# Softmax attention's head: the other heads' rows are stored after the first group's loads have landed

## The chip, the cores and the metric

One core of one Trainium2 chip runs the whole program. The metric is device time in microseconds (us) of one execution, lower being better; the time of a version is the median of several executions.

## The reference

The program is a chain of two layers, each attention and then a mixture of experts, on 2048 rows of 128 numbers. Only the second layer's attention is touched by the change. Cut to what matters:

```python
x = x + _L1_attn_ref(_layernorm(x, axis=-1), L1_attn_Wq, ...)
...
scale = 1.0 / np.sqrt(HD)
scores = jnp.einsum('bhsd,bhed->bhse', q, k) * scale
attn = jax.nn.softmax(scores, axis=-1)
out = jnp.einsum('bhse,bhed->bhsd', attn, v)
out = out.transpose(0, 2, 1, 3).reshape(b, l, e)
return out @ Wo.T + bo
```

Here q, k and v are x times a weight of 128 x 128 plus a bias, cut into 16 heads of 8 numbers, q and k turned by position-dependent angles (rope); x has 2 sequences of 1024 rows.

## The kernel before

The program runs four stages one after the other, with a barrier of all engines between them: delta-rule attention, experts, softmax attention, experts. The softmax attention lies in the profile from about 424 us to 809 us. `attn1_pe`, `attn1_dve`, `attn1_act`, `attn1_pool` and `attn1_sp` each write the instructions of one engine in the order in which it runs them; nothing is rescheduled. The engines meet at semaphores.

**The units.** q and k of 2048 positions are made in 8 units (`UNITS1`) of 512 positions each; unit 0 is k of positions 0 to 511, unit 1 is k of 512 to 1023, unit 2 is q of 0 to 511, unit 3 is q of 512 to 1023, all of the first sequence. Units 4 to 7 belong to the second sequence. Each value is cut into three bf16 thirds (semaphores `a1_h0`, `a1_h1`, `a1_r2` or `a1_r2d` say that a third is there), in the buffer `a1_part`, which has four slots: unit 4 writes where unit 0 lay, so ScalarE's `leading(4)` (line 1106) first waits until unit 0's stores have landed (line 1102).

**Through memory and back.** A unit has 16 heads by 8 numbers on the partitions; the score products want the 7 pair rows of a head on the partitions instead. SyncE (SP) therefore stores each third to a scratch tensor in main memory (`store`, line 1276) and loads it back in the other order (`load`, line 1283). The first group is heads 0 to 3: 32 partitions of each unit. The other heads are 96 partitions. The first FIRST = 3 units are stored in these two pieces, with semaphores `a1_sf0` to `a1_sf2` for the first group and `a1_st0` to `a1_st2` for the others; unit 3 goes as one piece. What a DMA queue holds is worked on in the background, but SP itself stands still at each `wait_ge`, and everything behind that wait in its program stands still too.

**SP's order before.** The nine stores of the first group, with two stores of the others' unit 0 among them; the three loads of the first group for maxima (224 KB each, semaphore `a1_first`); the remaining seven stores of the others' units 0 to 2; three stores of unit 3; then a wait for unit 3's stores, its load (`a1_second`), a wait for `a1_st0` to `a1_st2`, and eight loads of 448 KB (`a1_two0`, `a1_one1`, `a1_two1`, `a1_one2`; line 1283). Then `max_rows(0)`: four small stores of row maxima to `scr_m` (line 1295), a wait until they have landed, and a load of them into row positions of q (line 1297, semaphore `a1_mrow0`). Behind that come six more group loads and the stores of units 4 to 7.

**The loops.** TensorE computes 256 tiles of scores only for their row maxima (`max_half`, line 903, two products each; the first waits for `a1_first`), VectorE reduces each (line 1019). The first 26 tiles (AHEAD) run alone. From then on TensorE interleaves two tiles of maxima with four products of scores (`scores`, line 922) and, from the third unit on, eight products with the values (`values`, line 933). ScalarE takes the exponentials (line 1158). The maxima of 16 tiles are split by GpSimd (`split_rows`, lines 1227 to 1234) and turned by VectorE (line 1026, once after tile 19 and then every 16 tiles) for `max_rows`. The first `scores` waits for `a1_two0` and `a1_mrow0`.

Of the kernel before, what the change touches and what calls it, by code (L numbers as in the profile page):

```python
# [788 lines left out]
FIRST = 3  # L789
# [467 lines left out]
def attn1_sp(c):  # L1257
    nc, sp, m, S = c.nc, c.sp, c.mem, c.sem
    q, kk, mt = m["a1_q"], m["a1_k"], m["a1_mt"]
    scr = [nc.dram_tensor(f"scr_{n}", [NH, HD, PAIRS, T], BF16, kind="Internal").ap() for n in "qk"]  # L1260
    scr_m = nc.dram_tensor("scr_m", [2, 3, HG * 4, 4, 32], BF16, kind="Internal").ap()

    def store(n, third, heads, sem):

        what, b = UNITS1[n]
        if third < 2:
            sp.wait_ge(S(("a1_h0", "a1_h1")[third]), n + 1)
        elif n in DVE_UNITS:
            sp.wait_ge(S("a1_r2d"), n)
        else:  # L1270
            sp.wait_ge(S("a1_r2"), 1 if n == 0 else n - 1)
        at = slice(heads[0] * HD, heads[1] * HD)
        to = scr[what].rearrange("h d r t -> (h d) r t")[at, :, b * BLK:(b + 1) * BLK]
        rows = to[:, 3 * third:min(3 * third + 3, PAIRS), :] if what == 0 else to[:, third:PAIRS:3, :]
        part = m["a1_part"][at, n % 4, third, :].unsqueeze(1).broadcast_to([rows.shape[0], rows.shape[1], BLK])
        sp.dma_start(rows, part).then_inc(S(f"{sem}{n}"), 16)

    def store_all(n):
        for third in range(3):
            store(n, third, (0, NH), "a1_st")  # L1280

    def load(what, base, k, at, to, sem):
        sp.dma_start((q, kk)[what][base:base + KR, k, :, to],
                     scr[what][k * HG:(k + 1) * HG, :, :, at].rearrange("h d r t -> (d r) h t")).then_inc(S(sem), 16)

    def group(base, g, name):
        k, b = g % NG, g // NG
        for what in (1, 0):
            load(what, base, k, slice(b * L, (b + 1) * L), slice(0, L), name)

    def max_rows(e):
        g, qh = e // 2, e % 2
        sp.wait_ge(S("a1_mc"), e + 1)
        for r in range(4):
            sp.dma_start(scr_m[qh, :, :, r, :].rearrange("a i j -> i a j"), mt[32 * r:32 * r + 16]).then_inc(S("a1_ms"), 16)
        sp.wait_ge(S("a1_ms"), 64 * (e + 1))
        sp.dma_start(q[KR:KA, g % NG, :, qh * BLK:(qh + 1) * BLK],
                     scr_m[qh].rearrange("a (h t) r j -> a h (t r j)", h=HG)).then_inc(S(f"a1_mrow{qh}"), 16)

    block = [slice(b * BLK, (b + 1) * BLK) for b in range(QH)]  # L1300
    first, others = (0, HG), (HG, NH)
    for n in range(FIRST):
        for third in range(3):
            store(n, third, first, "a1_sf")
            if n == 0 and third < 2:
                store(n, third, others, "a1_st")
    for n in range(FIRST):
        sp.wait_ge(S(f"a1_sf{n}"), 48)
        what, b = UNITS1[n]
        load(what, S1B, 0, block[b], block[b], "a1_first")  # L1310
    store(0, 2, others, "a1_st")
    for n in range(1, FIRST):
        for third in range(3):
            store(n, third, others, "a1_st")
    store_all(3)
    sp.wait_ge(S("a1_st3"), 48)
    load(0, S1B, 0, block[1], block[1], "a1_second")
    for n in range(FIRST):
        sp.wait_ge(S(f"a1_st{n}"), 48)
    for g in range(NG):  # L1320
        group(0, g, f"a1_two{g}")
        if g + 1 < NG:
            group(S1B, g + 1, f"a1_one{g + 1}")
        if g == 1:
            max_rows(0)
    for n in range(4, 7):
        store_all(n)
    max_rows(1)
    store_all(7)
    max_rows(2)  # L1330
    for e in range(3, 2 * G):
        max_rows(e)
        if e == 3:
            for n in range(4, 8):
                sp.wait_ge(S(f"a1_st{n}"), 48)
        if e % 2 == 1 and e // 2 + 3 < G:
            g = e // 2 + 3
            sp.wait_ge(S("a1_s1"), 32 * (g - NG + 1))
            group(S1B, g, f"a1_one{g}")
            sp.wait_ge(S("a1_pv"), U * (g - NG + 1))  # L1340
            group(0, g, f"a1_two{g}")
    for qh in range(2):
        sp.wait_ge(S(f"a1_mrow{qh}"), 16 * G)


def attn1(c, w, x):
    attn1_sp(c)
    attn1_pe(c)
    attn1_act(c, x)
    attn1_dve(c, x)  # L1350
    attn1_pool(c, x)
    tables_sp(c, w, "f1", 1)
# [1232 lines left out]
```

## Time and profile before

| | us |
|---|---|
| three runs, median | 916.6 |
| three runs, lowest and highest | 915.05 and 917.56 |
| the profiled execution, its own time | 918.17 |
| the profiled execution, span from first to last instruction | 916.8 |
| VectorE busy | 689.2 (75% of the span) |
| TensorE busy | 747.2 (82%) |
| ScalarE busy | 499.5 (54%) |
| mean granted clock of TensorE | 0.887 of full speed |

The profiled execution took 918.17 us, of which 916.8 us are its span; that is 1.57 us above the median of the runs. The shares are averages over four stages with different limits, so what follows reads the stage of the change by itself. Positions such as "475.84" are microseconds from the start of the span.

### The profile page before, as it was taken

The numbers are of one execution on the slowest core, as the hardware profiler recorded it, in microseconds if no ns is written. First come the engines' busy times: TensorE is split into PE (matmuls) and PEld (weight loads), VectorE is DVE, ScalarE is ACT, GpSimd is POOL, SyncE is SP. The second block draws the span as 40 slices with busy tenths as digits, with TensorE's granted clock in tenths as the row PEclk, the third lists the DMA queues.
The fourth block names the chain that finished last, engine by engine and source line by source line (L and its number), as shares of the span: only waits on it lengthen the run. The fifth ranks groups of instructions, "written<-read, shape, count | busy, mean of one in ns | idle before, by whom it ended". The sixth has DMA issues, their size and how long they took to land. (4 is left out here: it accounts for less than half of the span.)

```text
span 916.8 us, 18626 instructions
## 1 busy us (share of the span) xinstructions
PE 747.2 (82%) x7061; PEld 364.4 (40%) x7062; DVE 689.2 (75%) x1378; ACT 499.5 (54%) x989; POOL 245.0 (27%) x297
## 2 busy tenths in 40 slices
PE   6999978988418999945887999999999999936880
PEld 3343256643317999943211222222222222225770
DVE  7868964457784555538796999999999998865765
ACT  4744412655403343434435888888888889821223
POOL 0130010323035666661552200000000100005773
PEclk9999979976658999977857999999999999956995
DMA  3530010000461111231878030303120000041113
GB/s 95 118 68 3 1 25 5 4 1 0 172 219 38 45 45 45 44 107 36 222 156 231 2 73 12 82 3 83 33 51 3 2 2 4 9 159 32 50 47 98
DMA packets 40624, 55.60 MB, mean 61 GB/s; under 512 B 12552, under 2 KB 28048, under 8 KB 39896
## 3 DMA queue, kind: packets, MB, share of 16 engines
q1 hardware_dynamic: 36568, 46.28, 18.8%
q0 software_dynamic: 3968, 8.13, 3.1%
q8 instruction: 57, 0.93, 0.4%
q14 instruction: 31, 0.25, 0.1%
HBM read 35.45 MB, written 14.75 MB: 55 GB/s over the span
## 5 line engine op out<-in xcount | busy, mean ns | idle before, releaser
L1019 DVE TENSOR_REDUCE arena<-psum 128x1 f32<-128x1024 f32 x256 | 300.7, 1216 | 24.0 <-PE psum L903 21.2
L1158 ACT ACTIVATE arena<-psum 128x512 f32<-128x512 f32 x512 | 265.9, 605 | 53.8 <-PE psum L922 53.7
L903 PE MATMUL psum<-arena 56*128 56x512 bf16 x512 | 179.2, 409 | 11.8 <-DVE arena L1019 10.2
L922 PE MATMUL psum<-arena 59*128 59x512 bf16 x512 | 155.8, 388 | 5.9 <-ACT arena L1158 3.7
L933 PE MATMUL psum<-arena 128*32 128x512 f32 x1024 | 138.1, 611 | 8.7 <-issue 8.7
L370 PE MATMUL psum<-arena 128*128 128x128 f32 x808 | 110.9, 290 | 7.9 <-DVE arena L424 7.2
L370 PEld LDWEIGHTS psum<-arena 128*128 128x128 f32 x808 | 99.0, 198 | 19.4 <-DVE arena L424 19.4
L922 PEld LDWEIGHTS psum<-arena 59*128 59x128 bf16 x512 | 38.3, 94 | 166.4 <-ACT arena L1158 141.3
L475 POOL DMA_INDIRECT rows_y<-arena x62 | 62.1, 1001 | 47.7 <-DVE arena L429 43.1
L1227 POOL TENSOR_SCALAR arena<-arena 128x16 f32<-128x16 f32 x16 | 4.1, 254 | 249.2 <-DVE arena L1019 249.0
L470 POOL DMA_INDIRECT arena<-rows_x,arena x62 | 60.9, 982 | 31.6 <-issue 16.8
L391 PE MATMUL psum<-arena 128*128 (+1 forms) x496 | 66.5, 278 | 0.9 <-ACT arena L454 0.8
L903 PEld LDWEIGHTS psum<-arena 56*128 56x128 bf16 x512 | 37.5, 95 | 71.3 <-DVE arena L1019 69.1
L391 PEld LDWEIGHTS psum<-arena 128*128 128x128 f32 x496 | 61.1, 194 | 1.2 <-DVE arena L429 0.9
L451 ACT ACTIVATE arena<-psum 128x512 f32<-128x512 f32 x39 | 23.3, 597 | 59.6 <-PE psum L370 59.6
L416 DVE TENSOR_TENSOR arena<-arena,psum 128x512 f32<-128x512 f32 x39 | 26.8, 686 | 33.4 <-PE psum L370 33.4
L412 DVE COPY arena<-arena 128x512 f32 x62 | 27.3, 440 | 26.6 <-issue 26.1
L448 ACT COPY arena<-arena 128x512 f32 x39 | 24.1, 619 | 34.8 <-DVE arena L303 19.5
L2242 PE MATMUL psum<-arena 128*32 128x512 f32 x352 | 40.8, 593 | 0.2 <-DMA arena<-arena 0.2
L933 PEld LDWEIGHTS psum<-arena 128*32 128x32 f32 x1024 | 20.6, 108 | 42.0 <-issue 38.5
L454 ACT ACTIVATE arena<-arena 128x512 f32<-128x512 f32 x23 | 14.5, 630 | 40.2 <-DVE arena L420 40.2
L1982 ACT ACTIVATE arena<-psum 128x64 f32<-128x64 f32 x32 | 7.2, 224 | 41.8 <-PE psum L2264 41.7
(316 smaller groups left out, 1068.0 us busy)
## 6 DMA issues: line engine op xcount, KB each, us to landing
arena<-scr_k SPq DMA_DIRECT2D x15, 448.0 KB
arena<-scr_q SPq DMA_DIRECT2D x15, 448.0 KB
arena<-in_f_up SPq DMA_DIRECT2D x1, 4096.0 KB, 13.8
arena<-rows_y SPq DMA_DIRECT2D x12, 256.0 KB, 5.5
scr_q<-arena SPq DMA_DIRECT2D x6, 384.0 KB, 3.8
arena<-in_f_down SPq DMA_DIRECT2D x1, 2048.0 KB, 20.1
rows_x<-xn SPq DMA_DIRECT2D x2, 1024.0 KB, 15.4
arena<-in_f_up SPq DMA_DIRECT2D x1, 2048.0 KB, 10.2
```

Of the source, the lines that this page charges most:

```text
L370: mm = pe.matmul(ps[:, bank, f * P:(f + 1) * P], w[:, a.pair, at], xt[:, a.pair, :], start=True, stop=True)
L391: mm = pe.matmul(ps[:, 5 + 2 * d.pair, 0:P], h[:, d.pair, f * P:(f + 1) * P], merged(wdown[:, ed, f * P:(f + 1) * P]), start=f == 0, stop= ...
L412: dve.tensor_copy(m["e_w"][:, x0.pair, 0:F], merged(m["e_up"][:, bass.ds(e, 1), 0:F])).then_inc(picked, 1)
L416: dve.tensor_tensor(h[:, u.pair, :], sg[:, u.pair, :], ps[:, 2 + u.pair, :], ALU.mult).then_inc(hidden, 1)
L470: pool.indirect_dma_start(xs[:, t % SLOTS, :], None, src, index).then_inc(landed[t % SLOTS], 16)
L475: pool.indirect_dma_start(dst, index, y[:, d.slot, :], None).then_inc(stored[d.slot], 16)
L903: mm = pe.matmul(ps[:, bank + half, :], q[rows, k, h, (qh * 4 + qt) * P:(qh * 4 + qt + 1) * P], kk[rows, k, h, half * BLK:(half + 1) * BLK ...
L922: pe.matmul(ps[:, score_bank(n), :], kk[0:KA, k, h, kb * P:(kb + 1) * P], q[0:KA, k, h, qh * BLK:(qh + 1) * BLK], start=True, stop=True).t ...
L933: mm = pe.matmul(ps[32 * h:32 * h + 32, 7, :], va[:, kb, (st % NG) * HG + h, :], pt[:, (u % 3) * HG + h, :], start=kb == 0, stop=kb == NTB ...
L1019: dve.tensor_reduce(mx[:, qh, h * 4 + qt:h * 4 + qt + 1], ps[:, bank:bank + 2, :].rearrange("p a b -> p (a b)"), X, ALU.max).then_inc(S("a ...
L1158: act.activation(pt[:, (u % 3) * HG + h, :], ps[:, score_bank(n), :], ACT.Exp, scale=float(HD) ** -0.5).then_inc(S("a1_exp"), 1)
L2242: mm = pe.matmul(ps[32 * h:32 * h + 32, fir_bank(n, i), :], m["a0_wfir"][:, (g0 + g) * H0 + h, :], v4[:, h, b, PAD + t0 - 4 * g:PAD + t0 - ...
```

## The change

The two stores of the other heads' unit 0 that lay among the first group's stores are taken out and put behind the loads, and SP waits for `a1_first` to reach 48, that is for all three loads of the first group to have landed, before it issues the first of these nine stores.

```diff
     for n in range(FIRST):
         for third in range(3):
             store(n, third, first, "a1_sf")
-            if n == 0 and third < 2:
-                store(n, third, others, "a1_st")
     for n in range(FIRST):
         sp.wait_ge(S(f"a1_sf{n}"), 48)
         what, b = UNITS1[n]
         load(what, S1B, 0, block[b], block[b], "a1_first")
-    store(0, 2, others, "a1_st")
-    for n in range(1, FIRST):
+    sp.wait_ge(S("a1_first"), 3 * 16)
+    for n in range(FIRST):
         for third in range(3):
             store(n, third, others, "a1_st")
     store_all(3)
```

No instruction of TensorE, VectorE, ScalarE or GpSimd changes or moves. On SP the beginning of the stage changes like this (line, transfer, partitions x pair rows x positions, and the semaphores waited for ahead of it; 32 partitions are the first group, 96 the others):

```order
 L1276 DMA scr_k<-arena 32x3x512 [waits barrier_Pool_Activation_PE_DVE_SP_release,a1_h0]
-L1276 DMA scr_k<-arena 96x3x512 [waits a1_h0]
 L1276 DMA scr_k<-arena 32x2x512 [waits a1_h1]
-L1276 DMA scr_k<-arena 96x2x512 [waits a1_h1]
 L1276 DMA scr_k<-arena 32x2x512 [waits a1_r2]
 L1276 DMA scr_k<-arena 32x3x512 [waits a1_h0]
```

The two stores of 96 partitions leave the place between the first group's; the nine stores of 32 partitions now follow one another. Behind the three loads SP's program has this:

```order
 L1283 DMA arena<-scr_k 56x4x512 [waits a1_sf1]
 L1283 DMA arena<-scr_q 56x4x512 [waits a1_sf2]
+L1276 DMA scr_k<-arena 96x3x512 [waits a1_h0,a1_first]
+L1276 DMA scr_k<-arena 96x2x512 [waits a1_h1]
 L1276 DMA scr_k<-arena 96x2x512 [waits a1_r2]
 L1276 DMA scr_k<-arena 96x3x512 [waits a1_h0]
```

The same two stores stand there now, the first of them behind the wait for `a1_first`, and all that follows in SP's program is behind that wait as well: twelve stores (nine of 96 partitions, three of 128) where ten stood, then the loads of the groups.

## Rows read from the trace of the kernel before

**Rows 1.** The page, part 5: busy, mean ns of one, idle before it.

```profile
L1019 DVE TENSOR_REDUCE arena<-psum 128x1 f32<-128x1024 f32 x256 | 300.7, 1216 | 24.0 <-PE psum L903 21.2
```

**Rows 2.** Windows: busy of PE, PEld, DVE, ACT, POOL; PEclk; DMA share; GB/s.

```profile
560.00:600.00 40.00, 38.17 (x261) 8.75 (x257) 38.15 (x35) 34.23 (x67) 2.89 (x11) 1.00 0.23 48
```

**Rows 3.** Timeline at the first scores: start, us, engine, line; idle before, releaser.

```profile
475.84 0.58 PE L922 MATMUL psum<-arena 59*128 59x512 bf16 x1 [2.07 <-DMA arena<-scr_m]
...
476.93 1.22 DVE L1019 TENSOR_REDUCE arena<-psum 128x1 f32<-128x1024 f32 x1 [1.89 <-PE psum L903]
```

**Rows 4.** Timeline of the SP queue: start, us of issuing, line, tensors, count.

```profile
437.51 0.88 SPq L1283 DMA_DIRECT2D arena<-scr_k  x2
438.64 0.31 SPq L1283 DMA_DIRECT2D arena<-scr_q  x1
438.99 2.96 SPq L1276 DMA_DIRECT2D scr_k<-arena  x4
442.00 4.51 SPq L1276 DMA_DIRECT2D scr_q<-arena  x6
449.76 0.33 SPq L1283 DMA_DIRECT2D arena<-scr_q  x1
...
468.12 1.71 SPq L1295 DMA_DIRECT2D scr_m<-arena  x4
473.33 0.84 SPq L1297 DMA_DIRECT2D arena<-scr_m  x1
...
500.59 1.52 SPq L1276 DMA_DIRECT2D scr_q<-arena  x3
```

**Rows 5.** Waits of the SP queue, 429 to 476: us, times, longest.

```profile
SPq L1297 <- DMA scr_m<-arena: 3.5, 1, 3.5
SPq L1283 <- DMA scr_q<-arena: 3.5, 2, 3.2
```

**Rows 6.** Windows of the transfers, columns as in rows 2.

```profile
440.00:442.00 2.00, 1.79 (x5) 0.87 (x5) 0.00 (x0) 1.36 (x3) 0.45 (x1) 1.00 1.07 210
...
443.00:446.00 3.00, 2.11 (x8) 0.52 (x7) 1.49 (x2) 2.78 (x5) 1.75 (x2) 1.00 1.07 372
446.00:449.00 3.00, 1.60 (x6) 0.22 (x4) 3.00 (x3) 0.68 (x2) 2.84 (x3) 1.00 0.99 349
...
451.00:460.00 9.00, 7.85 (x16) 1.02 (x16) 9.00 (x9) 0.62 (x1) 7.66 (x9) 0.50 0.89 200
460.00:470.00 10.00, 8.69 (x18) 1.03 (x16) 9.94 (x10) 1.23 (x2) 7.72 (x11) 0.50 0.93 191
...
502.00:504.00 2.00, 1.92 (x19) 0.41 (x11) 2.00 (x3) 1.67 (x5) 0.00 (x0) 1.00 1.06 375
```

**Rows 7.** Issues of scr_m stores, whole run (count, KB each, median us to landing).

```profile
scr_m<-arena SPq DMA_DIRECT2D x64, 3.0 KB, 1.4
```

**Rows 8.** Landing of the four scr_m stores, line 1295, 460 to 480.

```profile
DMA to landing us min/median/max: 3.4/3.6/3.9
```

**Rows 9.** Landing of the three stores of line 1276 issued from 500.59.

```profile
DMA to landing us min/median/max: 2.5/3.0/3.2
```

**Rows 10.** Timeline of TensorE where the first group's loads are awaited.

```profile
442.92 1.02 PE L878 MATMUL psum<-xnT,arena 128*128 128x512 f32 x2
443.87 1.03 PE L903 MATMUL psum<-arena 56*128 56x512 bf16 x4
```

**Rows 11.** Timeline rows of ScalarE, GpSimd and VectorE between the two.

```profile
449.46 0.62 ACT L1106 CAST arena<-arena 128x512 bf16<-128x512 f32 x1 [2.77 <-POOL arena L1209]
...
465.76 0.22 POOL L1234 TENSOR_TENSOR arena<-arena 128x16 bf16<-128x16 f32 x1
...
467.83 0.27 DVE L1026 STREAM_TRANSPOSE arena<-arena 128x96 bf16<-128x96 bf16 x1
```

**Rows 12.** Timeline of TensorE: line 933 at either clock.

```profile
481.52 1.93 PE L933 MATMUL psum<-arena 128*32 128x512 f32 x8
...
485.00 1.07 PE L933 MATMUL psum<-arena 128*32 128x512 f32 x8
```

## The prediction, made before the changed kernel was run

> **What bounds the kernel now.** I read the page's groups first. The costliest one is VectorE's reduction of maxima, 256 of them [rows 1], and late in the attention VectorE and TensorE are each busy 38.15 and 38.17 of 40 us [rows 2]. From the first scores on the stage is thus a train in which both are full; whatever delays the departure of that train delays its end, and the last stage stands behind a barrier. So the question is what sets the departure, and I read the timeline there. TensorE stands still for 2.07 us before the first scores at 475.84, released by the load of the row maxima, and VectorE for 1.89 us behind it [rows 3]. This is the wait that ends last, not the first group's loads.
>
> Following it back on SP's queue: the load of the maxima is issued at 473.33, though its four stores were issued from 468.12 on [rows 4], because SP waited 3.5 us for them to land [rows 5]. Over the run such a store lands in 1.4 us [rows 7], here it took 3.4 to 3.9 [rows 8]: it lies behind the group loads. Those are one load of 224 KB and eight of 448 KB, 3.9 MB, and the transfers ran at 200 and 191 GB/s without a gap from 451 to 470 [rows 6], which is the 20 us that 3.9 MB take. They start at 449.76 [rows 4], when the longest of SP's waits for stores, 3.2 us, ends [rows 5]: unit 3's stores have landed. So the chain is: others' and unit 3's stores landed, 20 us of loads, maxima stored and loaded, first scores. It has no slack at any link. The change acts on its first link.
>
> **The nine early stores, unchanged.** Each is held by the engine that makes its third, and SP issues the loads at 437.51 (two) and 438.64 [rows 4]. Removing two stores from between them frees queue time that SP would spend waiting for a third. I cost this at nothing; the last three first-group stores and the landing that releases the third load come after the removed ones have long drained. If that cover were absent it would be worth at most the two issues.
>
> **The loads of the first group.** I need their landing, which has no row of its own. It is before 443.87, when the first maximum starts, which waits for it [rows 10], and not far before: the transfers ran at 210 GB/s from 440 to 442, and at the 372 GB/s of stores alone from 443 on [rows 6]. I take 443.4. In the change nothing competes with them. By how much sooner, x, do they land? From below: nothing, if the rival transfers did not slow them. From above: three loads are 0.69 MB; at the 191 GB/s of the group loads that is 3.6 us, at the 375 GB/s seen for stores [rows 6] 1.8 us. With a start some 0.9 us after the issue at 437.51 and 0.6 us to complete (together the 1.5 us worked out below) they land at 442.6 or, at the fast rate, not before 440.8. So x lies between 0 and 2.6 us. The group loads are the same kind of transfer in the same direction, so I take a value near theirs, x = 0.7.
>
> **The wait and the twelve stores.** This is the term that counts. Before, seven stores of the others and three of unit 3 were issued from 438.99 and 442.00 [rows 4], so that they stood in the queues when the loads ended and ran at 372 and 349 GB/s from 443 to 449 [rows 6]. Now the first is issued when the loads have landed, and there are twelve: 672 KB for each of units 0 to 2 and 896 KB for unit 3, 2912 KB or 2.98 MB, where ten had 2432 KB. At 375 GB/s [rows 6] that is 7.95 us. What start and completion cost I take from three stores of 896 KB on empty queues: issued from 500.59 over 1.52 us [rows 4], a third one issued at about 501.6 and landed some 3.0 us later [rows 9], 504.55. That is 4.0 us, of which 0.917 MB at 375 GB/s are 2.45 us, so 1.5 us are fixed. Issuing is no bound: three took 1.52 us there, twelve would take 6.1. Unit 3's stores then land at 443.4 - x + 7.95 + 1.5 = 452.85 - x, against 449.76 before: 3.1 - x later, of which 1.3 us are the two moved stores (0.49 MB) and the rest the gap in which the queues are empty. With x = 0.7 that is **2.4 us**.
>
> **Who waits behind it.** The group loads start 2.4 us later and need their 20 us; the four small stores still lie behind them, the load of the maxima is issued near 475.7, and the first scores start near 478.2. TensorE's wait of 2.07 us becomes some 4.5, VectorE's of 1.89 some 4.3. Other waiters have room. ScalarE's `leading(4)` needs unit 0's stores and runs at 449.46, held by GpSimd; the first three of the twelve (0.69 MB, 1.8 us, plus 1.5) land at 446.7 - x, so 2.8 us remain, and behind those GpSimd's last step of the first split ends at 466.0 with VectorE's turn only at 467.83 [rows 11]. The 17th tile needs unit 3's load, issued near 452.2 then, and VectorE is there only at 443.87 + 16 x 1.216 = 463.3 [rows 1, 10], 11 us later. If x brings the first maximum forward, TensorE's own projections hold it until 442.92 + 1.02 = 443.94 [rows 10], so at most a tenth or two is won, and it would be spent in the wait before the first scores. So nothing of the possible gain reaches the end.
>
> **A rule weighed against this.** The rows show transfers at 210 GB/s where loads and a few stores met, and cannot tell whether the loads were slowed. The Trainium skill says in "DMA: Bandwidth & Descriptors", section "Queues, rings and completion order", that each of the DMA engines takes a queue's descriptors in ring order. By that rule stores issued behind the loads can't get ahead of them on a shared ring, so taking them away wins the loads little and x is near 0. By that rule the sum is the 919.7 of the second rival; no row here separates it from x = 0.7.
>
> **The sum.** The profiled execution's own 918.17 plus 2.4 is 920.6; it lies 1.57 above the median, so on the median 916.6 + 2.4 = **919.0 us**, 0.26% slower. What a measurement of this kernel can tell from no change is about 0.3%, 2.75 us, and the forecast lies just within.
>
> **Rivals.**
> - *Hidden* (chance 0.12): the delay is not passed on, because something I took for bound by the group loads isn't. Against it are the three waits in a row [rows 3, 5] and the landing of 3.6 us instead of 1.4 [rows 7, 8]. It gives 916.6, and if the first maximum's tenths count too, 916.4.
> - *Loads not slowed* (0.20), the slower side: x = 0. The whole 3.1 us arrive, 919.7, and it is beyond 0.3% wherever x is under 0.35 us. For it: a mixed rate of 210 GB/s is no lower than the 200 and 191 of group loads alone [rows 6].
> - *Clock* (0.15): the first scores run at half clock, 0.5, until shortly before 485: eight products of line 933 take 1.93 us there and 1.07 after [rows 12], and from one such burst to the next are 3.48 us (481.52 to 485.00) instead of the 2.4 that two reductions of maxima take [rows 1]. A longer standstill before the scores may bring one more slow burst, 1.1 us, or with a second one 2.2: 920.1 to 921.2.
> - *Faster* (0.05): the clock returns at once after the wait, which spares the slow burst and the one like it after the second stall of TensorE, 2 x 1.1 us, and x is at its upper bound of 2.6: 916.6 + 0.5 - 2.2 = 914.9. It decides the sign as soon as the two together exceed 3.1 us, and only with the scatter of the runs on top would it be below -0.3%.
> - My forecast, 0.48: x from 0.35 to 1.5, 918.2 to 919.4.
>
> **How the numbers follow.** Beyond +0.3% (919.35) lie the second rival (0.20 of it nearly whole), the clock (0.15) and a small part of my own case by the scatter of medians of some 1 us (0.07): slower 0.42 in all. Faster by over 0.3% is 0.05, the rest, 0.53, is within. The range takes the hidden case in at its low end and the clock case at its high end: 916.4 to 921.2.
>
> **What would show it.** Right: the same stage in the changed profile has the first large store of line 1276 issued near 442.8 with almost nothing on the queues for a microsecond before its data run; the load behind unit 3's stores near 452.2; the load of the maxima near 475.7; TensorE's wait before the first scores near 4.5 us; the first maximum where it was, within 0.3 us. Positions may be offset by what the stages ahead took. Wrong in x: the three loads to the first large store, before the 443.4 of my estimate by more than 1.5 or less than 0.35 us. Wrong in the chain: the load of the maxima is issued no later although the group loads start later. Wrong in the clock: more or fewer than one burst of line 933 near 1.9 us after the first scores.

## The result

The changed kernel took 921.35 us (median of 16 executions, 917.53 to 925.53), the kernel before, executed beside it, 917.53 us (median of 16, 915.05 to 920.54). The ratio is 1.0041 with a 95% interval of 1.0024 to 1.0058: 3.8 us slower, between 2.2 and 5.3. The prediction said 2.4 us and a range that ended at 921.2; the time lies just above it. Of the 2.3 us between the forecast time of 919.0 and 921.35, 0.9 are not the change's: the kernel before had a median of 917.53 in these executions and of 916.6 in the three that the prediction started from. The other 1.4 are the difference between 3.8 and 2.4.

The profiled executions alone would mislead. The span of the changed kernel's is 917.4 us against 916.8, but its attention also began 3.7 us earlier: the experts' stage ahead of it, in which nothing changed, happened to be that much shorter (from 200 to 300 us the granted clock was 0.74 there and 0.67 before). So I count from a point inside the stage that both versions reach in the same way, the issue of the first group's loads: 437.51 before [rows 4], 433.84 after. It lies 7.69 and 7.67 us behind the stage's first store (429.82 and 426.17).

The SP queue of the changed kernel (start, us of issuing, line, tensors, count) answers to [rows 4]:

```profile
433.84 0.87 SPq L1283 DMA_DIRECT2D arena<-scr_k  x2
434.99 0.31 SPq L1283 DMA_DIRECT2D arena<-scr_q  x1
439.78 3.63 SPq L1276 DMA_DIRECT2D scr_k<-arena  x6
443.45 4.47 SPq L1276 DMA_DIRECT2D scr_q<-arena  x6
450.97 0.33 SPq L1283 DMA_DIRECT2D arena<-scr_q  x1
...
464.58 1.71 SPq L1295 DMA_DIRECT2D scr_m<-arena  x4
474.41 0.84 SPq L1297 DMA_DIRECT2D arena<-scr_m  x1
```

SP sees the loads landed at 439.78, 5.9 us after their issue, and only then issues the first of the twelve stores. Unit 3's load follows at 450.97, 11.2 us later. The waits of SP between 429 and 480 (us in total, times, longest) answer to [rows 5]:

```profile
SPq L1297 <- DMA scr_m<-arena: 8.1, 1, 8.1
SPq L1276 <- DMA arena<-scr_q: 4.4, 1, 4.4
SPq L1283 <- DMA scr_q<-arena: 3.3, 2, 3.0
```

The second row is the wait that was added. The first is the one that the prediction followed: the maxima's small stores now lie behind the group loads for 8.1 us instead of 3.5. Their landing, which answers to [rows 8]:

```profile
DMA to landing us min/median/max: 8.5/8.6/8.7
```

TensorE and VectorE in the changed kernel (start, us, engine, line, count, in brackets the idle time before it and its releaser) answer to [rows 10] and [rows 3]:

```profile
440.22 1.03 PE L903 MATMUL psum<-arena 56*128 56x512 bf16 x4
```

```profile
476.94 0.58 PE L922 MATMUL psum<-arena 59*128 59x512 bf16 x1 [6.71 <-DMA arena<-scr_m]
```

```profile
478.02 5.93 DVE L1019 TENSOR_REDUCE arena<-psum 128x1 f32<-128x1024 f32 x5 [6.53 <-PE psum L903]
```

The first maximum starts 6.38 us after the loads' issue, before it was 443.87 - 437.51 = 6.36. That alone doesn't say when the loads landed, because TensorE's projections run right up to it in both kernels:

```profile
439.26 1.02 PE L878 MATMUL psum<-xnT,arena 128*128 128x512 f32 x2
```

The events of the semaphore `a1_first`, which stand in the trace, do say it: the last one comes 5.89 us after the loads' issue before and 5.93 after. The loads won nothing. The wait before the first scores is 6.71 us instead of 2.07. The page shows the same in its group of VectorE, whose idle time went from 24.0 us [rows 1] to 27.9, and in TensorE's group of scores:

```profile
L1019 DVE TENSOR_REDUCE arena<-psum 128x1 f32<-128x1024 f32 x256 | 301.0, 1217 | 27.9 <-PE psum L903 25.2
```

```profile
L922 PE MATMUL psum<-arena 59*128 59x512 bf16 x512 | 155.3, 387 | 10.9 <-DMA arena<-scr_m 6.7
```

Windows of the changed kernel (columns as in [rows 2], the last is GB/s) answer to [rows 6]:

```profile
435.00:437.00 2.00, 1.79 (x5) 0.63 (x4) 0.00 (x0) 2.00 (x4) 1.16 (x1) 1.00 0.84 209
437.00:439.00 2.00, 2.00 (x6) 0.93 (x5) 0.00 (x0) 1.10 (x3) 0.00 (x0) 1.00 0.71 136
439.00:440.00 1.00, 1.00 (x3) 0.21 (x2) 0.00 (x0) 1.00 (x3) 0.00 (x0) 1.00 0.02 5
440.00:447.00 7.00, 5.19 (x14) 0.92 (x14) 6.14 (x6) 3.43 (x6) 5.38 (x5) 0.72 0.90 278
447.00:450.00 3.00, 2.71 (x6) 0.26 (x4) 3.00 (x3) 0.62 (x1) 2.13 (x3) 0.50 0.97 336
...
460.00:470.00 10.00, 8.77 (x18) 1.03 (x16) 10.00 (x10) 1.90 (x2) 6.88 (x10) 0.50 0.93 188
```

With nothing beside them the loads ran at 209 and 136 GB/s, no faster than the 210 of before [rows 6], when stores were queued as well. Then a microsecond is empty. SP issues the twelve stores over 8.1 us, and in the seven shown they run at 278 GB/s, their start included, where stores had run at 372 and 349 before [rows 6].

### The profile page after: what moved, and what is told of

The parts are those of the page before. It is cut to its first block and busy times, and to the rows that moved or that the text cites. A ratio compares the mean times of both kernels' runs of the same rounds, so it can differ in the third digit from the quotient of the medians.

```text
span 917.4 us, 18628 instructions
## 1 busy us (share of the span) xinstructions
PE 742.6 (81%) x7062; PEld 360.9 (39%) x7062; DVE 690.1 (75%) x1378; ACT 499.6 (54%) x989; POOL 244.5 (27%) x297
## 5 line engine op out<-in xcount | busy, mean ns | idle before, releaser
L1019 DVE TENSOR_REDUCE arena<-psum 128x1 f32<-128x1024 f32 x256 | 301.0, 1217 | 27.9 <-PE psum L903 25.2
L922 PEld LDWEIGHTS psum<-arena 59*128 59x128 bf16 x512 | 38.3, 94 | 171.1 <-ACT arena L1158 141.7
```

Of the source, the lines that this page charges most:

```text
L922: pe.matmul(ps[:, score_bank(n), :], kk[0:KA, k, h, kb * P:(kb + 1) * P], q[0:KA, k, h, qh * BLK:(qh + 1) * BLK], start=True, stop=True).t ...
L1019: dve.tensor_reduce(mx[:, qh, h * 4 + qt:h * 4 + qt + 1], ps[:, bank:bank + 2, :].rearrange("p a b -> p (a b)"), X, ALU.max).then_inc(S("a ...
```

## The experiments

All positions in the table are counted from the issue of the first group's loads in the same execution: 437.51 before, 433.84 after, and in the order of the other rows 434.44, 433.94, 437.53, 433.84, 434.50, 436.87, 433.83, 437.40 and 435.61. "Turn" is VectorE's third turn of maxima (line 1026), by which the standstills of the stage's start are over; the stage's last product with the values (line 933) is as far from the kernel before as the third turn is, within 0.05 us in every version. In brackets stands the difference to the kernel before. The last column is the ratio of times with its interval, as us of 916.5.

| version | first maximum | group loads or unit 3's load issued | first scores | third turn | time, us |
|---|---|---|---|---|---|
| before | 6.36 | 12.25 | 38.33 | 79.55 | |
| after | 6.38 | 17.13 (+4.9) | 43.10 (+4.8) | 83.90 (+4.4) | +3.8 (2.2 to 5.3) |
| wait only | 6.37 | 16.18 (+3.9) | 41.77 (+3.4) | 83.02 (+3.5) | +2.6 (1.1 to 4.1) |
| move only | 6.37 | 13.83 (+1.6) | 40.08 (+1.8) | 82.31 (+2.8) | +1.4 (-0.4 to 3.1) |
| before, early maxima | 6.55 | 12.70 | 36.14 (-2.2) | 79.03 (-0.5) | -0.8 (-2.4 to 0.6) |
| after, early maxima | 6.37 | 17.25 | 35.97 (-2.4) | 78.91 (-0.6) | -1.4 (-2.8 to 0.1) |
| after, large stores first | 6.39 | 16.91 (+4.7) | 42.43 (+4.1) | 83.45 (+3.9) | +3.9 (2.1 to 5.8) |
| after, wait behind unit 0 | 6.36 | 15.07 (+2.8) | 40.92 (+2.6) | 82.58 (+3.0) | +1.8 (0.1 to 3.6) |
| after, two issuers | 6.46 | 15.77, groups 17.69 | 41.75 (+3.4) | 83.00 (+3.5) | +6.0 (3.4 to 8.5) |
| early maxima and split | 6.36 | 12.30 | 35.87 (-2.5) | 77.36 (-2.2) | -3.6 (-5.5 to -1.6) |
| loads behind as well | 6.52 | 12.65 | 36.11 (-2.2) | 71.65 (-7.9) | -9.2 (-10.8 to -7.5) |

**The wait alone.**

```diff
+    sp.wait_ge(S("a1_first"), 3 * 16)
     store(0, 2, others, "a1_st")
     for n in range(1, FIRST):
```

> The kernel before with the wait for the first group's loads alone: the two stores of unit 0 stay between the first group's, and the eight... that is the seven other large stores and unit 3's three are issued only when the loads have landed. In the changed kernel's trace the interval from the first store of the attention to the landing that lets the twelve stores go was 439.78 - 426.17 = 13.6 us, and from there to unit 3's load 450.97 - 439.78 = 11.2 us. Theory A (stores that are issued onto empty queues run below the 372 GB/s of stores that were queued before): ten stores need 2.49 MB at about 300 GB/s plus 1.5, so 9.8 us, against 6.4 before: the first scores come 3.4 us later than before, and the time is 3 to 3.5 us longer than before. Rival B (they run at full rate once started, and something else made the twelve slow): 1.5 + 6.6 = 8.1 us, 1.8 us later than before.

The SP queue of this version:

```profile
440.69 2.01 SPq L1276 DMA_DIRECT2D scr_k<-arena  x4
442.75 4.82 SPq L1276 DMA_DIRECT2D scr_q<-arena  x6
450.62 0.33 SPq L1283 DMA_DIRECT2D arena<-scr_q  x1
```

From the first of the ten stores to unit 3's load are 9.93 us; 9.8 was theory A, 8.1 the rival. The window inside them:

```profile
442.00:447.00 5.00, 3.46 (x8) 0.49 (x8) 5.00 (x5) 2.00 (x4) 4.04 (x4) 0.67 0.94 290
```

The wait by itself accounts for 3.4 of the 4.8 us by which the first scores come later.

**The move alone.**

```diff
-    sp.wait_ge(S("a1_first"), 3 * 16)
     for n in range(FIRST):
         for third in range(3):
             store(n, third, others, "a1_st")
```

> The changed kernel without its wait: the two stores stand behind the loads, and all twelve are issued at once. Theory A (the order of a queue keeps the stores behind the loads, and stores that stand queued run at full rate): the loads land as in both kernels, 13.6 us after the attention's first store, and all twelve run at 370 GB/s behind them: 0.49 MB more than before, 1.3 us later first scores, 1.3 us longer. Rival B (the twelve are slow because of what the other engines do at that time, or because there are more of them): below 320 GB/s here too, and 2.5 us or more longer. Rival C (stores queued behind the loads slow the loads): the first maximum comes later than before by some tenths.

Here all twelve stores are issued while the loads are under way. Queue and window:

```profile
435.43 4.87 SPq L1276 DMA_DIRECT2D scr_k<-arena  x6
440.34 4.47 SPq L1276 DMA_DIRECT2D scr_q<-arena  x6
447.77 0.33 SPq L1283 DMA_DIRECT2D arena<-scr_q  x1
```

```profile
439.00:445.00 6.00, 4.48 (x14) 0.97 (x12) 4.05 (x4) 3.90 (x7) 4.15 (x4) 0.84 1.05 361
```

The same twelve stores of the changed kernel run at 361 GB/s. So neither their number nor the engines' work at that time is what slows them, and 0.49 MB more cost 1.6 us, near the reckoned 1.3. Rival B falls. Rival C can't be judged by the first maximum (6.37 us), ahead of which the projections run here too, but by the last event of `a1_first`: it comes 6.18 us after the loads' issue with all twelve stores queued behind, 6.00 with three (the wait behind unit 0), 5.89 to 6.42 in the four versions with ten, and 5.93 to 6.32 in the five where nothing is issued before the loads have landed. So stores queued behind the loads take nothing from them that stands out of this scatter, and rival C falls. The first maximum never comes before 6.36, where the projections end, and at 6.46 to 6.55 where the loads land at 6.32 to 6.42.

From the first scores to the third turn the delay grew here, from 1.8 to 2.8 us, as the table shows. It goes with TensorE's clock, of which the next experiments show more: the clock rose to full at 484.1, 10 us after the first scores, where in the kernel before it had been 8.2.

**Early maxima, on both kernels.** In `attn1_sp`, for the kernel before and in the same way for the changed one:

```diff
-    for g in range(NG):
+    for g in range(NG - 1):
         group(0, g, f"a1_two{g}")
-        if g + 1 < NG:
+        if g + 2 < NG:
             group(S1B, g + 1, f"a1_one{g + 1}")
-        if g == 1:
+        if g == 0:
             max_rows(0)
...
     max_rows(2)
+    group(S1B, NG - 1, f"a1_one{NG - 1}")
+    group(0, NG - 1, f"a1_two{NG - 1}")
```

> The kernel before with another order of SP's queue behind unit 3's stores: the first maxima are stored and loaded after four of the group loads instead of eight, and the last two group loads come after the third maxima. Theory (the first scores wait for the maxima, which wait behind the group loads): the four small stores land in under 2 us, TensorE's wait of 2.07 us ahead of the first scores is gone, and the time is 1.5 to 2 us shorter. Rival (the first scores are held by something else): the same time as before.

> The changed kernel with the same new order of SP's queue as in the kernel before with early maxima. Theory (the change's delay reaches the end through the group loads and the maxima alone): with only four group loads ahead of the maxima they end some 5 us later than in the other, near the time at which the maxima are stored, so the first scores wait little or not, and the time is within 0.5 us of the other's; both are faster than the kernel before. Rival (the delay is passed on in another way): some 4 us slower than the other.

The first scores of the two versions, of the kernel before first, and the landing of the small stores, the same row in both:

```profile
473.67 0.58 PE L922 MATMUL psum<-arena 59*128 59x512 bf16 x1
```

```profile
469.81 0.58 PE L922 MATMUL psum<-arena 59*128 59x512 bf16 x1
```

```profile
DMA to landing us min/median/max: 1.3/1.4/1.4
```

The rows of the first scores carry no idle time any more, and the small stores land in 1.4 us. Although the changed kernel's group loads start 4.6 us later in this order too, its first scores come at 35.97 us and those of the other at 36.14: nothing of the change's delay is left. So the whole delay went through the group loads and the maxima behind them, and the rival falls. Against the kernel before the times are lower by 0.8 and 1.4 us, with intervals that both reach zero; expected was 1.5 to 2 for the first. The reason stands in the column of the third turn: of 2.2 us only 0.5 are left there. TensorE's clock stayed at half for longer. In the kernel before it rose at 484.0, 8.2 us after the first scores; here at 484.4, 10.7 us after, as this window shows:

```profile
480.00:484.00 4.00, 4.00 (x20) 0.71 (x24) 2.36 (x3) 1.78 (x5) 2.40 (x2) 0.50 0.99 213
484.00:486.00 2.00, 1.80 (x14) 0.29 (x6) 1.59 (x3) 1.09 (x4) 0.00 (x0) 0.90 0.99 199
```

From 480 to 484 VectorE is busy 2.36 of 4 us with TensorE full at clock 0.50. Part of a second burst with the values falls into the slow stretch: it takes 1.43 us, where before it took 1.07 [rows 12].

```profile
483.62 1.43 PE L933 MATMUL psum<-arena 128*32 128x512 f32 x8
```

By the second turn 1.0 us of the 2.2 is left. There VectorE stands still a second time, the clock falls again, and it is back 6.8 us after that turn (501.5) instead of 5.4 (501.1), and by the third turn another 0.5 us is gone.

All eleven traces follow one pattern, counted from the first group's loads: where the first scores came at 35.9 to 38.3 us, the clock rose at 46.0 to 46.9; where they came at 40.1 to 43.1, it rose at 50.1 to 50.3. So a delay of the first scores doesn't arrive at the third turn one for one: 1.8 us became 2.8, 2.6 became 3.0, and 4.8 became 4.4.

**Why the twelve stores take 11.2 us**, where 9.45 were reckoned. Three versions of the changed kernel. In the first, two of unit 3's stores go first; in the second the wait stands behind unit 0's three stores; in the third ScalarE issues unit 3's stores.

```diff
     sp.wait_ge(S("a1_first"), 3 * 16)
+    store(3, 0, (0, NH), "a1_st")
+    store(3, 1, (0, NH), "a1_st")
     for n in range(FIRST):
         for third in range(3):
             store(n, third, others, "a1_st")
-    store_all(3)
+    store(3, 2, (0, NH), "a1_st")
```

> The changed kernel with two of unit 3's stores (128 partitions, 384 KB each) issued first behind the wait, then the nine of the other heads (96 partitions), then unit 3's last. Bytes and count are those of the changed kernel, where 11.2 us lay between the first of the twelve and unit 3's load and the transfers ran at about 300 KB per us while SP was still issuing. Theory A1 (stores run slowly while the queue holds little ahead of them; two large ones fill it at once, as issuing them takes only 0.45 us each): the interval falls to 9.5 to 10 us, with 360 KB per us nearly throughout. Rival A2 (transfers run slowly as long as SP is issuing beside them and little is queued, whatever the size): it stays at 11 us or more. Against the kernel before: first scores 3 us later by A1, 4.7 by A2.

It took 10.95 us from the first of the twelve to unit 3's load. Its windows:

```profile
442.00:443.00 1.00, 0.19 (x1) 0.11 (x2) 1.00 (x2) 0.78 (x2) 0.92 (x2) 1.00 1.08 383
443.00:449.00 6.00, 4.90 (x11) 0.64 (x10) 6.00 (x6) 1.75 (x4) 4.37 (x4) 0.55 1.00 311
```

The two large ones run at 383 GB/s, all that follow at 311 until SP is through with issuing at 449.4. A1 falls; filling the queue at once doesn't help.

These windows hold a difference that no experiment was made for. The slow rates belong to the nine stores of 96 partitions. Unit 3's, of 128 partitions, ran fast even where they met empty queues: at 383 here and at 375 in the three stores from 500.59 [rows 6, 9]. The changed kernel itself shows both kinds, the second window being the first that has unit 3's data:

```profile
447.00:448.00 1.00, 0.82 (x3) 0.04 (x2) 1.00 (x2) 0.25 (x1) 0.72 (x1) 0.50 0.96 319
448.00:449.00 1.00, 1.00 (x2) 0.09 (x2) 1.00 (x1) 0.37 (x1) 0.49 (x1) 0.50 1.08 382
```

Stores of 96 partitions ran at 361 to 375 too, in the move alone and in the kernel before, where they had been queued behind loads. So in these traces the slow rate shows only where both come together, the smaller stores and the issue behind a wait. That is a comparison of rows and no test: twelve stores of 128 partitions behind the wait were not run.

```diff
-    sp.wait_ge(S("a1_first"), 3 * 16)
     for n in range(FIRST):
         for third in range(3):
             store(n, third, others, "a1_st")
+        if n == 0:
+            sp.wait_ge(S("a1_first"), 3 * 16)
     store_all(3)
```

> The changed kernel with the wait moved three stores down: unit 0's stores of the other heads stand behind the loads in the queue, the nine that follow are issued when the loads have landed. The chain theory with the order of the queue: the first maximum comes no later than in any other version (14.05 us after the attention's first store), because queued stores take nothing from the loads; the stores' data run from the loads' end on without a gap, so the first scores come between those of the kernel with the wait removed (1.7 us later than before) and the changed kernel (4.75 later): about 2.5 later. Rival (the loads win by having the queues alone): the first maximum is earlier in the changed kernel than here.

```profile
438.37 5.86 SPq L1276 DMA_DIRECT2D scr_k<-arena  x6
```

```profile
443.23 1.03 PE L903 MATMUL psum<-arena 56*128 56x512 bf16 x4
```

The first maximum is where the projections let it start, 6.36 us after the loads' issue, and the first scores are 2.6 us later than before, as expected.

```diff
-    store_all(3)
...
     biased(7)
+    act.wait_ge(S("a1_h0"), 4)
+    act.wait_ge(S("a1_h1"), 4)
+    act.wait_ge(S("a1_r2"), 2)
...
+    for third in range(3):
...
+        act.dma_start(rows, part).then_inc(S("a1_st3"), 16)
     for n in (4, 5):
         leading(n)
```

> The changed kernel with unit 3's three stores issued by ScalarE behind its last biased copy instead of by SP, so that SP issues nine behind the wait. In the changed kernel SP spent 8.1 us on issuing the twelve (0.68 each instead of the 0.51 that I reckoned with), and unit 3's load came 3.0 us after the end of that, 11.2 in all. Theory I (issuing is what bounds: the wait puts 8.1 us of it behind the loads, where before it ran beside them): SP's nine take about 6.2 us and ScalarE's three run beside them, so the load comes 9.3 to 10 us after the first of the twelve, and the first scores 3 to 3.5 us later than in the kernel before instead of 4.75. Rival T (the transfers bound, issuing is only held back by them): the interval stays at 11 us and each store takes longer to issue.

SP's and ScalarE's issues (the new lines of the file shift line 1276 to 1284 and 1283 to 1291):

```profile
440.17 5.00 SPq L1284 DMA_DIRECT2D scr_k<-arena  x6
445.21 3.73 SPq L1284 DMA_DIRECT2D scr_q<-arena  x3
449.60 0.31 SPq L1291 DMA_DIRECT2D arena<-scr_q  x1
451.52 0.31 SPq L1291 DMA_DIRECT2D arena<-scr_k  x1
```

```profile
441.90 1.10 ACTq L1155 DMA_DIRECT2D scr_q<-arena  x2
443.03 2.35 ACTq L1155 DMA_DIRECT2D scr_q<-arena  x1
```

Unit 3's load comes 9.4 us after the first store, within theory I, but that is the wrong mark here: unit 3's stores have a queue of their own and overtake. All twelve have landed only when the group loads start at 451.52, 11.35 us after the first; in the changed kernel all had landed when unit 3's load was issued at 450.97, 11.19 after the first. Nine issues took SP 8.8 us instead of 6.2, and one of ScalarE's 2.35. So a second issuing engine wins nothing for the twelve, and each store takes longer to issue, as rival T says: issuing by SP alone isn't what bounds them. That the first scores still come at +3.4 and not at +4.8 has its place in the loads: from the first group load to the maxima's load are 21.3 us here and 23.0 in the changed kernel. Most of this difference is unit 3's load: it was issued 1.9 us ahead of the group loads here and 0.4 us in the changed kernel, so less of it lay in their way (by estimate its 0.23 MB are 1.2 us at the 191 GB/s of [rows 6]). What makes the stores slow I could not settle. The time of this version has a wide interval, 3.4 to 8.5 us above the kernel before, of which its trace explains 3.5.

**Two steps further.** The delay showed a train that passes every standstill on. Every trace has a second one, 5.4 us of VectorE before its second turn, released by GpSimd. On top of early maxima for the kernel before:

```diff
     rotate(6)
-    rotate(7)
     split_rows(1)
+    rotate(7)
...
-        if u == 4:
+        if u == 5:
             leading(7)
-        if u == 5:
+        if u == 6:
             following(7)
```

> The kernel before with early maxima (as in e3), and in addition GpSimd splits the second 16 maxima before it turns unit 7, and ScalarE takes unit 7's first two thirds one unit later. In every trace so far VectorE stands still for 5.4 us ahead of its second turn (line 1026), released by GpSimd's split. Theory (the train of maxima and scores passes every standstill on to the end): that wait falls under 1 us and the time is 3.5 to 5 us below the kernel with early maxima alone, near 910 to 912. Rival (the standstill is made up by what is ahead of it): no faster than the kernel with early maxima.

VectorE's rows (the second turn, and the wait that took its place):

```profile
488.48 0.27 DVE L1026 STREAM_TRANSPOSE arena<-arena 128x96 bf16<-128x96 bf16 x1
...
500.65 1.22 DVE L1019 TENSOR_REDUCE arena<-psum 128x1 f32<-128x1024 f32 x1 [4.83 <-PE psum L903]
```

The turn has no wait ahead of it, but 4.83 us came back at 500.65: the second maxima's small stores were issued sooner and now met the transfers that lie ahead of them. The time was 912.4 us. By the ratios of the table that is 2.8 us below early maxima alone (3.4 by the medians), short of the expected 3.5 to 5. So the last step takes one pair of loads out of their way:

```diff
-        group(0, g, f"a1_two{g}")
+        if g < 2:
+            group(0, g, f"a1_two{g}")
...
     max_rows(2)
+    group(0, 2, "a1_two2")
     group(S1B, NG - 1, f"a1_one{NG - 1}")
```

> The kernel with early maxima and the earlier split, and one more pair of group loads (the third group's for scores) moved behind the third maxima. There VectorE stood still for 4.8 us at 500.65, and the second maxima's small stores, issued from 491.2, were followed by their load only at 497.2: they lay behind group loads and unit 4 to 6's stores. Theory (any bulk transfer ahead of the maxima's small stores is passed on to the train): 0.9 MB less ahead of them, 4.7 us at 195 KB per us, so they land near 493, the standstill is nearly gone, and the time is 3 to 4 us shorter, near 908 to 910. Rival (another standstill takes its place): no shorter by more than 1 us.

```profile
487.27 0.27 DVE L1026 STREAM_TRANSPOSE arena<-arena 128x96 bf16<-128x96 bf16 x1
487.47 13.14 DVE L1019 TENSOR_REDUCE arena<-psum 128x1 f32<-128x1024 f32 x11
```

Eleven reductions follow the second turn in one row. The small stores, issued at 487.57, were followed by their load at 490.59, 3.0 us later instead of 6.0. The time was 907.26 us (median of 6, 906.6 to 908.92), a ratio of 0.990 (0.9882 to 0.9918) to the kernel before: faster than both kernels of this case, by 9.2 us than the one before. The step was worth 5.6 us by the ratios, more than the expected 3 to 4, and the traces show where more came from. In the other ten, TensorE's clock fell to half a second time for 6.8 us, in the kernel before from 494.3 to 501.1; with the standstills around the second turn gone, it stayed up. The kernel before first, then this version:

```profile
495.00:501.00 6.00, 3.89 (x17) 0.61 (x17) 3.74 (x4) 1.02 (x2) 0.49 (x3) 0.50 0.46 156
```

```profile
483.00:500.00 17.00, 15.77 (x112) 3.92 (x112) 16.25 (x16) 15.20 (x31) 6.68 (x8) 1.00 0.48 166
```

## Why the prediction was too low

- **What bounds the stage** was right: nothing that the first maximum could have gained would count, and the first scores held by the maxima behind the group loads. Early maxima on both kernels show that this chain carries the whole delay. The group loads took what they had taken: 449.76 to 473.33 is 23.6 us before, 450.97 to 474.41 is 23.4 after.
- **"The loads of the first group"**, x = 0.7 us: wrong, x is 0 within the scatter. The second rival had it. The estimated landing before, 443.4, was right (5.89 us after the issue; the trace's last event of `a1_first` says the same). But x was taken from the 191 GB/s of the group loads, and these three, alone, ran at 209 and then 136. They landed 5.93 us after their issue, not 5.2. The Trainium skill says in "DMA: Bandwidth & Descriptors", section "Queues, rings and completion order", that each DMA engine consumes descriptors in ring order. These traces agree with what the prediction made of that rule, x near 0: the loads land between 5.89 and 6.42 us after their issue, and no later with stores queued behind them than without.
- **"The wait and the twelve stores"**, 7.95 + 1.5 = 9.45 us from the first issue to unit 3's load: this is the step that failed. It took 11.19 us. The start was as reckoned, 0.9 us from the issue to the first data (the window 440 to 441 has a DMA share of 0.32); the 375 GB/s wasn't. With 1.5 us fixed, 2.98 MB in the remaining 9.7 us are 308 GB/s, an estimate; the windows show 290 in the wait alone and 311 in the version with large ones first. I took the rate from stores that had been queued before their data ran, and from three of 128 partitions; nine of the twelve have 96 and were issued behind a wait. The sentence "Issuing is no bound" rested on 0.51 us for each; it was 0.68, though a second issuing engine didn't shorten the whole.
- **The sum** of the two: 0.7 and 1.7 us on top of 2.4 make the 4.8 us by which the first scores came later, twice the forecast.
- **What arrives at the end**: 4.4 us at the third turn, and 3.8 (2.2 to 5.3) in the time. The time came nearer to the forecast than the first scores did, and part of that is luck. The clock rival didn't happen in the changed kernel: its slow stretch after the first scores was shorter, 7.2 us instead of 8.2, with one slow burst as before, and 0.4 us of the 4.8 were given back. Had the first scores come near the forecast 2.4 us, the clock would probably have gone the rival's way, if by less than its 1.1 us: in the version with the wait behind unit 0 they came 2.6 us later, and 3.0 arrived at the third turn.
- **Who else waits** was right: `leading(4)` and the split were not delayed. `leading(4)` (line 1106) started 11.95 us after the loads' issue before and 11.96 after, and SP issued the maxima's stores at 468.12 - 437.51 = 30.6 and 464.58 - 433.84 = 30.7 us.

The range was too narrow at the top because only one term with unknown size was given bounds, and because it left no room for another median of the kernel before, which alone moved the time by 0.9 us. The transfer rate of the twelve stores, measured on other stores in another state of the queue, was taken as known.

## What to carry to other kernels

In this kernel, a wait that kept transfers back until earlier ones had landed cost more than the gap: the held ones started on empty queues, were issued while they ran, and ran more slowly. Before adding such a wait, see whether the earlier ones lose anything at all; here they lost nothing. Where small transfers that an engine waits for lie behind bulk ones in a queue, the order of the queue can be worth more than what fills it. The change cost the kernel before 3.8 us; early maxima, the earlier split and one pair of loads moved behind the maxima, together, won it 9.2.

## What the runs showed of the hardware

- Loads into 56 partitions ran at 188 to 200 GB/s over ten microseconds of group loads, and the first group's three at 209 and 136 with nothing beside them. Stores to main memory ran at 349 to 372 when they stood queued. Transfers of either kind are not one rate.
- Stores of 96 partitions, issued after a wait onto empty queues and fed while they ran, ran at 290 to 311 GB/s. It isn't their number (twelve at 361 in the move alone), nor does it help to put large ones ahead of them or to let a second engine issue three: all had landed 11.35 us after the first instead of 11.19. Stores of 128 partitions ran at 375 to 383 on empty queues. What makes the difference is open.
- The stretch at half clock after the first scores was 7.2 us in the changed kernel, 8.2 before and 10.7 with early maxima. Where the first scores came within 38.3 us of the first group's loads, the clock rose at 46.0 to 46.9; where they came at 40.1 or later, at 50.1 to 50.3. Of a standstill of 2.2 us that was taken away, 1.7 were given back there and around the second slow stretch, of 6.8 us. Ten of the eleven traces have that second stretch; the last version, which has no standstill ahead of it, doesn't.
